# The last group in three parts: images 12 and 13, image 14 alone, image 15 alone, and a new order of events

## What is computed

```python
x = x + _L0_conv_ref(_gn(x), ...)      # group norm, 2x upsampling with a 12-tap filter, leaky relu, 12-tap filter, 2x downsampling
t = _to_tokens(x)                      # 1024 tokens of 32 channels per image
t = t + _L1_attn_ref(_ln_t(t), ...)    # causal attention, softmax over 1024 keys, per image
t = t + _L1_ffn_ref(_ln_t(t), ...)     # 16 experts; each takes its 8 best tokens of an image
```

## Time and profile before

| | |
|---|---|
| median of 3 runs | 427.67 us (427.49 to 428.02) |
| the profiled execution | 429.69 us, its span 427.8 us |
| TensorE, VectorE, ScalarE, GpSimd busy | 83%, 76%, 60%, 56% of the span |
| mean granted TensorE clock | 0.892 of 2.4 GHz |

### The profile page before, as it was taken

How to read it: one execution, slowest core, us unless ns; L and a number is a source line. 1 busy time by engine, 2 the same in 40 slices (tenths; PEclk the granted TensorE clock), 3 DMA queues, 4 the chain that set the end, 5 groups by cost and what they waited for, 6 DMA issues and landing times.

```text
span 427.8 us, 7761 instructions
## 1 busy us (share of the span) xinstructions
PE 356.7 (83%) x3022; PEld 267.0 (62%) x3022; DVE 323.8 (76%) x551; ACT 257.0 (60%) x342; POOL 238.3 (56%) x138
## 2 busy tenths in 40 slices
PE   1199899999999997989988979898788697854995
PEld 1088777677778584748766847486654345443785
DVE  3878957887778778987787789777979888773631
ACT  0122424788998867589766675997485856811500
POOL 5405543485895996774755967747558735132000
PEclk9999979999999998999998989999898886855555
DMA  4700000000000000000000000000410000000122
GB/s 110 180 1 2 0 2 2 2 3 1 3 2 2 2 2 1 2 2 0 2 2 2 0 3 0 2 2 2 90 13 2 1 0 2 2 0 0 51 73 75
DMA packets 16432, 6.82 MB, mean 16 GB/s; under 512 B 6479, under 2 KB 16269, under 8 KB 16397
## 3 DMA queue, kind: packets, MB, share of 16 engines
q1 hardware_dynamic: 13680, 5.68, 5.7%
q10 hardware_dynamic: 2717, 0.66, 0.9%
HBM read 4.16 MB, written 2.11 MB: 15 GB/s over the span
## 4 chain that ended last, share of the span: by engine, by line
PE 55%; DVE 18%; issue 9%; ACT 9%; DMA 3%; POOL 2%; SPq 1%; POOLq 1%; ACTq 1%; DVEq 0%
PE psB L839 10%; PE psA L839 9%; PE psB L965 5%; PE psB L947 5%; PE psA L932 4%; DVE negmax L709 4%; PE psA L1008 4%; PE psA L972 3%; ACT e L552 3%; ACT Pp L553 3%; PE psB L979 3%; DVE Pp L376 2%; PE psA L829 2%; DVE t_all L734 2%; PE psA L925 2%
## 5 line engine op out<-in xcount | busy, mean ns | idle before, releaser
L376 POOL TENSOR_TENSOR Pp<-e,Pp 128x1024 f16<-128x1024 f32 x45 | 99.1, 2203 | 30.8 <-ACT Pp L553 30.6
L709 DVE TENSOR_REDUCE negmax<-psA 128x1 f32<-128x512 f32 (+7 forms) x128 | 91.0, 750 | 21.2 <-PE psA L935 20.8
L552 ACT ACTIVATE e<-psB 128x1024 f32<-128x1024 f32 (+1 forms) x80 | 76.1, 951 | 11.0 <-PE psB L947 8.6
L553 ACT ACTIVATE Pp<-psB 128x1024 f16<-128x1024 f32 (+1 forms) x80 | 76.7, 958 | 0.0
L839 PE MATMUL psB<-xin,UU 128*128 128x224 f16 (+1 forms) x480 | 60.1, 287 | 2.1 <-ACT oT L557 1.8
L947 PE MATMUL psB<-yQ,zK 128*128 128x512 f16 (+1 forms) x192 | 51.6, 347 | 7.4 <-ACT Pp L553 4.6
L839 PE MATMUL psA<-y,DD 128*128 128x224 f16 (+1 forms) x480 | 55.2, 273 | 1.5 <-DVE negmax L709 1.5
L839 PEld LDWEIGHTS psB<-xin,UU 128*128 128x128 f16 x480 | 49.1, 103 | 11.0 <-ACT oT L557 2.1
L932 PE MATMUL psA<-zK,yQ 128*128 128x512 f16 x192 | 47.7, 337 | 7.2 <-DVE tF L682 5.7
L839 PEld LDWEIGHTS psA<-y,DD 128*128 128x128 f16 x480 | 46.6, 98 | 7.2 <-DVE negmax L709 1.9
L441 POOL TENSOR_TENSOR zrstd<-zrstd,power 128x8 f32<-128x8 f32 x16 | 30.8, 1924 | 30.4 <-DVE zrstd L689 30.1
(11 more groups left out here) (154 smaller groups left out, 626.4 us busy)
## 6 DMA issues: line engine op xcount, KB each, us to landing
x_all<-in_x_dram SPq DMA_DIRECT2D x4, 512.0 KB, 4.7
out_dram<-x_all SPq DMA_DIRECT2D x8, 256.0 KB, 2.3
y<-in_L_ffn_weight_dram SPq DMA_DIRECT2D x3, 256.0 KB, 4.2
yQ<-rows SPq DMA_DIRECT2D x32, 2.0 KB
Pp<-filter_tables ACTq DMA_DIRECT2D x4, 121.9 KB, 3.1
cst<-shape_constants SPq DMA_DIRECT2D x1, 326.5 KB, 4.3
xin<-in_L_ffn_weight_dram SPq DMA_DIRECT2D x1, 256.0 KB, 4.8
Pp<-filter_tables ACTq DMA_DIRECT2D x1, 120.0 KB, 3.3
```

The lines of the kernel that those rows point to most:

```text
L376: return engine.tensor_tensor(Pp[:, n % 2, 1, o:o + N], e32[:, (NU * n + i) % 3, 0:N], Pp[:, n % 2, 0, o:o + N], ALU.subtract)
L552: nc.scalar.activation(e32[:, m % 3, 0:N], slot(e)[:, 0:N], ACT.Exp)
L553: nc.scalar.activation(Pp[:, n % 2, 0, UOFF[e[2]]:UOFF[e[2]] + N], slot(e)[:, 0:N], ACT.Exp).then_inc(b_drained, 1)
L709: ins = nc.vector.tensor_reduce(negmax[:, n % 2, m - 1:m], s[:, at:at + P * m], X, ALU.max, negate=True)
```

## The change

The last group has three parts instead of two. `proj`, `mean` and `dev` of group 3 now are 0 (images 12 and 13), 1 (image 14) and 2 (image 15). The work per image is the same; parts 1 and 2 have half of the columns. `LAST_IMAGE` takes the place of `LAST_PAIR`, so that the additions and products of image 14 are GpSimd's and those of image 15 VectorE's. The whole table `STEP` and the order in `LAST` are new. The diff, cut to its core:

```diff
-LAST_PAIR = (G - 1, 1)
+LAST_IMAGE = (G - 1, 2)
+ALONE = ("proj", "mean", "dev")
...
 def group(late, name, *more):
 
-    return lambda t: (name, (t - late) // GB) + more if (t - late) % GB == 0 and 0 <= t - late < B else None
+    groups = G - 1 if name in ALONE and more == (1,) else G
+    return lambda t: (name, (t - late) // GB) + more if (t - late) % GB == 0 and 0 <= t - late < GB * groups else None
...
+def span_of(n, i):
+
+    return ((0, 2), (2, 3), (3, 4))[i] if n == G - 1 else ((0, 2), (2, 4))[i]
...
-STEP = [batch(-1, "low", 1), group(5, "proj", 1), batch(3, "down"), once(-3, "gn_mean", 1), once(3, "image", 2),
...
+STEP = [batch(1, "score", 2), once(-1, "image_low", 1), batch(3, "z_rstd"), once(3, "image_low", 2),
...
-LAST = [("hidden", 0), ("dev", G - 1, 1), ("uT", G - 1), ("experts", 0), ("logits", G - 1), ("turned", 0),
-        ("logit_max", G - 1), ("select", G - 1), ("logit_exp", G - 1), ("scatter", 1), ("route", G - 1),
-        ("scatter", 2), ("wT", G - 1), ("pool", G - 1), ("scatter", 0), ("hidden", 1), ("experts", 1), ("turned", 1),
-        ("scatter", G - 1)]
+LAST = [("proj", G - 1, 2), ("hidden", 0), ("mean", G - 1, 2), ("experts", 0), ("dev", G - 1, 2), ("turned", 0),
+        ("uT", G - 1), ("scatter", 1), ("logit_max", G - 1), ("logits", G - 1), ("select", G - 1), ("scatter", 2),
+        ("logit_exp", G - 1), ("route", G - 1), ("wT", G - 1), ("scatter", 0), ("pool", G - 1), ("hidden", 1),
+        ("experts", 1), ("turned", 1), ("scatter", G - 1)]
...
                 elif name == "proj":
-                    pe.wait_ge(b_drained, BU["pv", GB * n + 2 * e[2] + 1] + 1)
-                    for k in range(KT):
+                    first, last = span_of(*e[1:])
+                    pe.wait_ge(b_drained, BU["pv", GB * n + last - 1] + 1)
+                    for k in range(KT // 2 * (last - first)):
```

More of the change, by code:

```diff
@@ L99, in group @@
 def group(late, name, *more):
-    return lambda t: (name, (t - late) // GB) + more if (t - late) % GB == 0 and 0 <= t - late < B else None
-def once(step, name, n):
-    return lambda t: (name, n) if t == step else None
-FIRST = [("xT", 0), ("gn_mean", 0), ("gn_var", 0), ("U", 0), ("normalise", 0), ("image", 0), ("UU", 0), ("image_low", 0)]
-STEP = [batch(-1, "low", 1), group(5, "proj", 1), batch(3, "down"), once(-3, "gn_mean", 1), once(3, "image", 2),
[L127 to L137, removed]
-        batch(0, "prob", 2), group(3, "mean", 0), once(-3, "normalise", 1), group(7, "pool"), group(5, "uT")]
@@ L722, in _ @@
                         dve.wait_ge(b_filled, BU["logits", n - 1] + 1)
[L723 to L725 removed]
+                    first, last = span_of(*e[1:])
+                    tiles = KT // 2 * (last - first)
+                    sv = s.rearrange("p (k d) -> p k d", k=KT)[:, 0:tiles]
@@ L728, in _ @@
                 elif name == "mean":
+                    first, last = span_of(*e[1:])
                     dve.wait_ge(a_drained, A["proj", n, e[2]] + 1)
-                    if n >= 1:
+                    if n >= 1 and e[1:] != LAST_IMAGE:
                         dve.wait_ge(t2_centred, 2 * n + e[2] - 1)
-                    dve.wait_ge(b_drained, BU["tok", GB * n + 2 * e[2] + 1] + 1)
-                    v = t2_all[:, n, 2 * BC * e[2]:2 * BC * (e[2] + 1)]
-                    link(nc.vector.tensor_tensor(v, v, att[:, 2 * BC * e[2]:2 * BC * (e[2] + 1)], ALU.add))
@@ L735, in _ @@
-                    link(nc.vector.tensor_reduce(nmean[:, e[2], :], v.rearrange("p (n c) -> p n c", c=C), X, ALU.add))
-                    nc.vector.tensor_scalar(nmean[:, e[2], :], nmean[:, e[2], :], -1.0 / C, None, ALU.mult).then_inc(t2_mean, 1)
-                    if e[1:] == LAST_PAIR:
-                        dve.wait_ge(t2_mean, 2 * G)
+                    dve.wait_ge(b_drained, BU["tok", GB * n + last - 1] + 1)
+                    v = t2_all[:, n, BC * first:BC * last]
+                    shift = nmean[:, e[2], 0:KT * (last - first)]
```

79 lines of the change are left out of this document (53 added, 26 removed).

## The result

The changed kernel takes 410.45 us (median of 3 runs, 410.31 to 410.60) against 427.67 before: a ratio of 0.959, with a 95% interval of 0.955 to 0.964. It is 17.2 us faster where 9.2 us were predicted. Executions more than 1.5% above the fastest of their kernel, which had a lower granted clock, are left out of every ratio here.

What follows compares the result with a forecast made beforehand. TensorE (83% busy) was taken to lose 25.5 us in steps 0 to 11, mostly where VectorE stood beside GpSimd; VectorE bounded steps 12 to 15. Terms -6.5 - 2 - 1.2 + 0.5 = -9.2 from 427.67 gave 418.5 us, range 408 to 431.

Steps and rivals of the forecast that it cites:

- fewer meetings in front of TensorE's waits: Steps 5, 7, 9 and 11: VectorE held up beside GpSimd, some 20 us lost, of which 9 were left.
- ScalarE's lag: Steps 0 to 11: TensorE waits for ScalarE to free banks for `score` and `up`, 0.55 us per step, +6.6 us.
- Rival C: Steady steps: ScalarE frees `prob` 0's banks late, 1.4 us per step, giving 430 to 436 us; chance 0.16.
- The three meetings at 3 us each: Steps 0 to 11: GpSimd and VectorE still meet, 9 us lost in all, bounds 0 and 20.
- The other tight places: `score` (t+2, 1) waits for `proj` 0's product, 0.8 us three times, +2.4; `proj` 1 waits for ScalarE, 0.5 twice, +1.
- Steps 12 to 15: The stage from `prob` (12, 0) to the last `pv`: -2 us, between -5 and +2.
- The two terms behind the attention: The last layer norm, -1.2 us, and the stretch from `uT` to the end, +0.5 us.
- rival E: Last stage: the clock rises as idle time before `uT` shortens, 10 us less than forecast, 408 us; chance 0.02.
- D: Steps 5 to 15: nearly all losses go with TensorE at full clock, 401 to 408 us; chance 0.10.
- B: Bad steps: meetings only change place and keep their 20 us, 429 to 430 or 425 to 427 us; chance 0.22.

Runs made afterwards that it cites:

- the run with the start alone: The kernel before with only the events ahead of `prob` (0, 0) in the new order, `gn_var` 2 and `normalise` 2 a step later: ratio 0.994.
- the short `low`: GpSimd's `low` takes only 8 columns per unit from image 2 on: in the kernel before 413.2 us (0.966), in the changed kernel 403.5 us (0.945).

## Why the prediction came out as it did

The direction was right, and the 410.45 us lie in the range. The mechanism, fewer meetings in front of TensorE's waits, was right for steps 5, 7 and 9, but it gave 5.3 us of the 19.2 between the two profiles. The prediction was 8 us short. In the profiles that is 10 us (19.2 less 9.2), 2.0 of which are before's profiled execution above its median: 5.1 us at the start, 3.8 in steps 0 to 11, 1.0 in steps 12 to 15, and some tenths behind them. There are four reasons.

1. **The start had no term.** The change part by part began at the steady steps, and the sum counted nothing ahead of `prob` (0, 0). Measured: 5.1 us less there, 2.0 of them paid back in steps 0 and 1 (14.63 and 18.05 us instead of 14.61 and 16.11, where `normalise` 2 now stands), 3.1 us net, and 2.8 net in the run with the start alone; beside a start of 77.1 us both are 1.5 us less. This is the stage that was left out.
2. **ScalarE's lag was mis-sized.** The term was +6.6 us, 0.55 per step. The plain step 3 takes 16.21 us, beside 16.12 for before's plain step 1, and in the stretch of the waits above TensorE waited for ScalarE 1.3 us in all at `up` and `tok`; no wait at `prob` 1 is among them. The step that failed is that ScalarE's queue ahead of `prob` 0 "holds as much as before". In before's timeline ScalarE was still at `prob` 4 of the image ahead when step 2 began at 109.32 us, and came to `prob` 0 at 110.97, 1.65 us late:

```profile
110.01 0.66 ACT L552 ACTIVATE e<-psB 128x512 f32<-128x512 f32 x1
110.49 0.67 ACT L553 ACTIVATE Pp<-psB 128x512 f16<-128x512 f32 x1
110.97 1.11 ACT L552 ACTIVATE e<-psB 128x1024 f32<-128x1024 f32 x1
```

   In the changed kernel `zK`, `tok` and three `score` stand between `prob` 4 and the next `prob` 0, and ScalarE comes to `prob` 0 of step 3 at 124.59, 0.69 us behind the step's start at 123.90. It frees the banks at 126.42, 0.7 us before TensorE wants them at 127.13:

```profile
123.90 0.38 PE L967 MATMUL psB<-yQ,zK 128*128 128x512 f16 x1
...
124.59 1.02 ACT L563 ACTIVATE e<-psB 128x1024 f32<-128x1024 f32 x1
...
126.42 1.03 ACT L552 ACTIVATE yQ<-psA 128x1024 f16<-128x1024 f32 x1
...
127.13 0.39 PE L967 MATMUL psB<-yQ,zK 128*128 128x512 f16 x1
```

   The two excerpts are of different steps, and step 2 carries group work in before. Over steps 0 to 11 ScalarE comes to `prob` 0 0.69 to 1.65 us late in before, and 4.5 in steps 5 and 9; in the changed kernel it is 0.69 to 1.21 in every step. Like for like, step 2 goes from 1.65 to 0.69 and step 3 from 0.90 to 0.69. So the 3.46 us of the earlier trace rows were also not typical. Rival C, built on the same lag, falls with it.
3. **The meetings were 11.9 us and not 20, and fell to 6.6 and not 9.** The saving in this term was 5.3 us instead of 11. The prediction put the whole loss of the four bad steps down to the meetings; with the short `low` step 11 of before stays at 19.29 us. The three meetings at 3 us each that I left were in the main one of 5.9 us in step 6, as the run with `image_low` moved shows.
4. **The other tight places.** Behind the drain of `proj` 0 the waits were 0, 4.1 and 0.8 us instead of three times 0.8 (2.4). The last is the predicted size; the 4.1 is the meeting, counted above. `proj` 1 waited for ScalarE's copy twice 0.74 us: 1.5 instead of 1.

So the lost time in steps 0 to 11 is 223.67 less 208.4, 15.3 us, where 19.0 was forecast. The sum came this near partly by luck, as two errors had opposite signs. The meetings saved 5.7 us less than forecast. All other losses together were to grow by 4.5 us (from 5.5 to the 10.0 of the tight places), and they fell by 5.0, from 13.6 to 8.7, which is 9.5 us better. ScalarE's term explains 5.3 of those 9.5; the rest stays open. Steps 12 to 15 came out 1 us better than forecast, which is within what the clock of that stage alone changes: in kernels with this order and this split they took 61.55 to 65.34 us. Two sums of the prediction are also off, without weight: 1.03 us of `yQ`'s copy and as much again make 2.06 us per step and not 1.4, so that the upper bound of ScalarE's term was +25 us, and 16.3 + 1.1 + 3.95 + 3.65 + 1.5 make 26.5 and not 26.6.

The two terms behind the attention were right by their own steps. The layer norm of image 14 runs ahead of that of image 15 on VectorE's queue and takes up most of what the shorter operations give: the second root is over at 369.87 us, 6.5 us after the second projection ended at 363.37. And `scatter` 1 ahead of `logits` (376.38 us, 5.9 behind `uT`, instead of 4.1) makes `wT` wait for `route`, as foreseen. In the changed kernel's timeline:

```profile
368.24 1.63 POOL L449 TENSOR_TENSOR urstd<-urstd,power 128x8 f32<-128x8 f32 x1 [1.36 <-DVE urstd L767]
...
372.35 4.10 PE L1029 MATMUL psA<-obd,xF_all 64*128 64x128 f32 x16
...
376.38 3.67 PE L1000 MATMUL psB<-uT,gateT 128*64 128x512 f32 x4
...
386.95 1.19 PE L849 MATMUL psA<-cst,xF_all 64*128 64x64 f32 x8 [2.87 <-DVE xF_all L787]
```

The clock stood at 0.50 in that stage, so rival E did not happen. D (nearly all losses go) did not happen either, as 15.3 of the 25.5 us remain. B (the meetings only change their place) is refuted as to its time by the four kernels with and without the short `low`, but it describes step 6, and GpSimd's longer `low`.

## What to carry to other kernels

A table that every engine walks through in order moves the share of *all* engines with an event. Before moving one, read for each engine which instruction it issues there, what that waits for, and what is queued behind it; the moves of `mean` and of `gn_var` beside `normalise` were lost that way, on ScalarE and on VectorE. Put no VectorE instruction that may meet GpSimd right ahead of a drain for which TensorE waits: behind the drain the same pair cost next to nothing in the one case tried (step 7 was 0.2 us longer). And price every stage that the new order touches, the one before the loop included.
